# One kernel of graph layers: the projection matrices get a load semaphore of their own, and orders, banks and rows are new

## What is computed

```
x = layernorm(x + L0(x))   # q,k,v = x @ w.T + b; 4 heads; softmax(mask(q k / sqrt(32))) v; @ wo.T + bo
x = layernorm(x + L1(x))   # h = x W; softmax over leaky_relu(s_i + d_j), masked; times h
x = layernorm(x + L2(x))   # the same with 8 heads and a log prior; @ W_out.T
x = layernorm(x + L3(x))   # relu(x w + b); attention of width 256 without mask, elu; relu(x w + b);
                           # attention of width 128 with mask, elu, sums
```

## Time and profile before

| what | value |
|---|---|
| median of 3 runs | 1070.28 us (1068.1, 1070.28, 1076.06) |
| the profiled execution, its own time | 1069.56 us |
| its span, first to last instruction | 1067.7 us |
| TensorE busy | 999.2 us (94%) |
| VectorE busy | 910.9 us (85%) |
| ScalarE busy | 763.6 us (72%) |
| GpSimd busy | 403.2 us (38%) |
| mean granted clock of TensorE | 0.991 |

### The profile page before, as it was taken

The page is one execution under the profiler, slowest core; times in us unless marked ns, Lnnn a source line. Parts: engine busy times, 40 slices in busy tenths (PEclk is TensorE's granted clock), DMA queues, the critical chain, the costliest instruction groups (busy, mean ns, idle before and its releaser), DMA issues. The chain is left out here.

```text
span 1067.7 us, 25731 instructions
## 1 busy us (share of the span) xinstructions
PE 999.2 (94%) x8649; PEld 731.7 (69%) x8649; DVE 910.9 (85%) x2499; ACT 763.6 (72%) x2022; POOL 403.2 (38%) x660
## 2 busy tenths in 40 slices
PE   7999999999999999999999999999999999998995
PEld 4776666775667677676868677776867576856774
DVE  3988998889899798998899999788889996899654
ACT  4789875785888687788877789797866836544653
POOL 1013333250444562434736371653535272320111
PEclk9999999999999999999999999999999999999998
DMA  4001111021212120312203130310202120320000
GB/s 128 2 22 43 60 64 60 21 91 45 68 44 70 52 87 27 102 42 75 73 27 93 41 113 11 92 41 32 82 26 87 32 82 1 101 70 22 11 10 21
DMA packets 41530, 57.89 MB, mean 54 GB/s; under 512 B 12728, under 2 KB 15288, under 8 KB 41400
## 3 DMA queue, kind: packets, MB, share of 16 engines
q1 hardware_dynamic: 40536, 55.98, 17.2%
q10 hardware_dynamic: 864, 0.26, 0.1%
HBM read 51.12 MB, written 5.11 MB: 53 GB/s over the span
## 5 line engine op out<-in xcount | busy, mean ns | idle before, releaser
L1329 DVE SCALAR_TENSOR_TENSOR P<-row,t2e,mask_t 128x512 f32<-128x512 f32 x512 | 367.4, 776 | 13.3 <-PE bank L689 10.9
L856 ACT ACTIVATE probs<-probs,low 128x512 f32<-128x512 f32 x256 | 185.6, 727 | 46.4 <-DVE low L1128 45.5
L1128 DVE CUSTOM_DVE_ANT_0 probs<-bank,mask_add 128x512 f32<-128x512 f32 x256 | 170.1, 675 | 10.2 <-PE bank L582 10.1
L867 ACT ACTIVATE probs_t<-bank 128x512 f32<-128x512 f32 x232 | 136.3, 606 | 19.8 <-PE bank L590 19.4
L590 PE MATMUL bank<-ident,probs 128*128 128x128 f32 x1024 | 139.6, 277 | 7.0 <-ACT probs L856 5.5
L590 PEld LDWEIGHTS bank<-ident,probs 128*128 128x128 f32 x1024 | 112.8, 141 | 44.4 <-ACT probs L856 25.1
L902 ACT ACTIVATE x<-x,shift_l,rstd_l 128x128 f32<-128x128 f32 x256 | 105.3, 487 | 47.9 <-POOL shift_l L1486 47.5
L1471 POOL TENSOR_TENSOR rstd_l<-mv_l,ln_eps 128x4 f32<-128x4 f32 x64 | 19.8, 309 | 303.8 <-DVE mv_l L1197 303.8
L734 PE MATMUL bank<-t,l_P 128*128 128x258 f32 x512 | 119.3, 387 | 4.9 <-DVE low L1128 2.1
L689 PE MATMUL bank<-P,GH 128*32 128x512 f32 x1024 | 118.2, 602 | 4.5 <-issue 2.3
L734 PEld LDWEIGHTS bank<-t,l_P 128*128 128x128 f32 x512 | 95.9, 192 | 20.9 <-DVE low L1128 2.3
(11 more groups left out here) (179 smaller groups left out, 1958.3 us busy)
## 6 DMA issues: line engine op xcount, KB each, us to landing
row<-l_line SPq DMA_DIRECT2D x158, 256.0 KB, 3.8
x_in<-in_x SPq DMA_DIRECT2D x16, 256.0 KB, 2.6
out<-x SPq DMA_DIRECT2D x15, 256.0 KB, 2.0
row<-l3b_line SPq DMA_DIRECT2D x10, 256.0 KB, 3.0
l_P<-in_adj SPq DMA_DIRECT2D x4, 256.0 KB, 4.5
l_line<-turned SPq DMA_DIRECT2D x26, 16.0 KB
l_line<-l_turned SPq DMA_DIRECT2D x20, 16.0 KB
w_fc<-in_L_gnn_W_fc SPq DMA_DIRECT2D x1, 256.0 KB, 3.8
```

Source lines behind the costliest of these rows:

```text
L856: act.activation(e, e, ACT.Exp, bias=low0[:, m:m + 1], scale=-1.0, accum_out=g.of(den0)[:, m:m + 1])\
L867: act.activation(probs_t[c % 2][:, h, :, :].rearrange("p j n -> p (j n)"), ps("l0_t", g, m)[:, :], ACT.Copy)\
L1128: dve.tensor_tensor_reduce(probs[c % 2][:, h, :], ps("l0_s", g, m)[:, :], mask_add[:, c, :], 1.0, LOWEST, ALU.add, ALU.min, low0[:, m:m + ...
L1329: last = dve.scalar_tensor_tensor(P2[:, h % GROUP2, j, :], row("l2_spread", g, h)[:, :], g.of(t2e)[:, j, h:h + 1], mask_t[:, j, :], ALU.ma ...
```

## The change

The three matrices are loaded first, then the bias of q, the bias of k, and the bias of v. `proj_in` now counts only the three matrices, and TensorE's `proj_T` waits for those three. The biases of q and k count on a new semaphore, which ScalarE waits for ahead of scaling the bias of q; the bias of v counts on another, which VectorE waits for in `l0_v` of graph 0.

The tables `ORDER`, `BANK_OF_USE` and `ROW_OF_USE` are replaced. Each string has the same turns as before, except that TensorE has 63 warm-up turns where it had 65. A warm-up turn now stands on both sides of `proj_T`. The first 12 turns of ScalarE, 6 of VectorE, 18 of GpSimd and 15 of SyncE are unchanged, and so are the last 163 of TensorE (41 of them warm-up turns), 122 of ScalarE, 151 of VectorE, 33 of GpSimd and 21 of SyncE. The kernel has no table of durations, so only the orders show that part of the change. The diff, with some lines of two of the strings and without the rest of the tables:

```diff
--- before.py
+++ after.py
     "pe":
-        "Z0Z0a010Z0b0c0d0e0e0f0f0f0a1f020b1c1f0e0g0f0f0d1Z0Z0Z0Z0Z0Z0Z0Z0Z0000000f000Z0e0f0f0g0f0f0e1f0g0f0f0"
...
-        "b4c4g3t0f3f3u0f3f3d4o1j2p1p1k2e4g3q1k2f4e4f4Z0r1t0f4f4e4u0f4l2f4f4i3v0f4e4w0g4f4f4f4f4g4a5g4f4b5c5d5"
-        "f4x0Z0Z0j3y0y0k3k3f4t1l3z0z0z0z0n2f4A0u1e5g4n2f5B0i4f5f5t1Z0u1C0o2f5C0C0p2p2C0j4e5q2k4k4v1g5r2w1D0n3"
...
-        "ybrdFaFaffzbzbzbzbefffffffAbfftcGagfgfucffffffvcffwcnegfhfneifZ0Z0tdCbxcCbCbCbjfJakfkfudJaoetdDbpepe"
-        "DblfIaudEbycycmfFbFbzczczcqezcreGbvdAcwdnfBcnfZ0Z0CcxdCcCcCcZ0Z0Z0Z0ofJbpfpfJbDcDcqfZ0terfIbEcydydue"
...
+        "Z0Z0a0Z010Z0b0c0d0e0e0f0f0f0a1f020b1f0c1e0f0g0f0d1Z0Z0Z0Z0Z0Z0Z0Z0Z0000000f000g0e0f0f0f0f0e1f0g0f0f0"
...
+        "f3d4f3t0g3f3f3u0f3j2o1e4p1p1f3k2k2f4g3q1e4f4f4f4t0r1e4u0i3f4l2f4f4v0f4g4w0e4f4f4f4f4j3g4k3k3f4x0a5g4"
+        "f4y0y0l3f4f4z0z0z0g4b5z0t1A0n2c5u1n2i4e5B0d5f5f5Z0Z0Z0C0C0C0o2C0p2p2e5f5f5q2t1r2e5j4f5u1f5f5k4k4f5v1"
...
+        "ffffzbzbzbzbefgfAbfffffffftcgfgfucffffffffGaZ0gfhfvcZ0wcneneiftdCbxcCbCbCbjfJakfkfudJatdDboeDblfudpe"
+        "peIaEbycycmfFbFbzczczcqezcreGbvdAcwdnfBcnfZ0Z0CcxdCcCcCcZ0Z0Z0Z0ofJbpfpfJbDcDcqfZ0terfIbEcydydueFcFc"
...
     "dve":
-        "00a0b0b0b0b0c00020b0c0b030b04010b050c0a10060b0c0b000b0b0c0b0b0b0c0b0b1b1b1c0d0c0e0b1b1b1b1f0b1c1c1g0"
...
+        "00a0b0b0b0b000c0b020c0b030b04010b0c050a100c0b060b000b0b0b0c0b0b0c0b0b1b1b1c0d0c0e0b1b1b1b1f0c1b1c1g0"
...
@@ -328,7 +328,7 @@
         row_filled = [sem(f"row_filled{r}") for r in range(ROWS)]
         x_loaded = [sem(f"x_loaded{q}") for q in range(2)]
         stored = [sem(f"stored{q}") for q in range(2)]
-        for name, n in [("proj_in", 6 * 16), ("out_in", 3 * 16), ("l1_in", 2 * 16), ("l2_in", 4 * 16), ("l3_in", 9 * 16), ("add_mask", C), ("one_mask", 1),
+        for name, n in [("proj_in", 3 * 16), ("bias_qk_in", 2 * 16), ("bias_v_in", 16), ("out_in", 3 * 16), ("l1_in", 2 * 16), ("l2_in", 4 * 16), ("l3_in", 9 * 16), ("add_mask", C), ("one_mask", 1),
                         ("fold1", 1), ("fold2", 1), ("fold3", 1), ("prior_in", 1), ("prior_exp", 1), ("prior_ln", 1),
                         ("prior_out", 1), ("x_biased", 1), ("bias_q_made", 1), ("exp0", 16), ("den0_safe", 1), ("rden0_made", 1),
                         ("l2_c4", 1), ("dmax8_diag", 1), ("small2_made", 2), ("exp2", 3), ("gh2", 1), ("rden2_made", 2), ("p2_made", HEADS2),
@@ -762,7 +762,7 @@
                 last.then_inc(filled("l3_r", g), 1)
 
             stages = {
-                "mask_T": mask_T, "proj_T": turn_raw("proj_T", ("wq", "wk", "wv"), "proj_in", 6 * 16),
+                "mask_T": mask_T, "proj_T": turn_raw("proj_T", ("wq", "wk", "wv"), "proj_in", 3 * 16),
                 "out_T": turn_raw("out_T", ("wo", "w_out"), "out_in", 3 * 16), "l0_xT": to_T("l0_xT", lambda g: g.of(x_in), lambda g: pe.wait_ge(g.of(x_loaded), 16 * (g.i // 2) + 16)),
                 "l0_q": l0_qk("q"), "l0_k": l0_qk("k"), "l0_v": l0_v, "l0_s": l0_s, "l0_t": l0_t, "l0_pv": l0_pv,
                 "l0_rd": l0_rd, "l0_y": l0_y,
@@ -795,13 +795,11 @@
         @block.scalar
         def _(act):
             def proj_load(g, k):
-                loaded = signal["proj_in"]
-                for n, key in (("wq", "L0_gnn_wq"), ("wk", "L0_gnn_wk")):
-                    act.dma_start(rawf[:, RAW[n] * D:(RAW[n] + 1) * D], w[key]).then_inc(loaded, 16)
-                act.dma_start(bias_q[:, 0:1], w["L0_gnn_bq"].rearrange("(p o) -> p o", o=1)).then_inc(loaded, 16)
-                act.dma_start(bias_k[:, :], w["L0_gnn_bk"].rearrange("(p o) -> p o", o=1)).then_inc(loaded, 16)
-                act.dma_start(rawf[:, RAW["wv"] * D:(RAW["wv"] + 1) * D], w["L0_gnn_wv"]).then_inc(loaded, 16)
-                act.dma_start(bias_v[:, :], everywhere(w["L0_gnn_bv"], D)).then_inc(loaded, 16)
+                for n, key in (("wq", "L0_gnn_wq"), ("wk", "L0_gnn_wk"), ("wv", "L0_gnn_wv")):
+                    act.dma_start(rawf[:, RAW[n] * D:(RAW[n] + 1) * D], w[key]).then_inc(signal["proj_in"], 16)
+                act.dma_start(bias_q[:, 0:1], w["L0_gnn_bq"].rearrange("(p o) -> p o", o=1)).then_inc(signal["bias_qk_in"], 16)
+                act.dma_start(bias_k[:, :], w["L0_gnn_bk"].rearrange("(p o) -> p o", o=1)).then_inc(signal["bias_qk_in"], 16)
+                act.dma_start(bias_v[:, :], everywhere(w["L0_gnn_bv"], D)).then_inc(signal["bias_v_in"], 16)
                 act.preload_act_table_set("natural_log_exp_and_others")
 
             def raw_out(stage, names):
@@ -814,7 +812,7 @@
 
             def proj_t(g, k):
                 raw_out("proj_T", ("wq", "wk", "wv"))(g, k)
-                act.wait_ge(*sig("proj_in", g, 6 * 16))
+                act.wait_ge(*sig("bias_qk_in", g, 2 * 16))
                 act.activation(bias_q[:, 1:2], bias_q[:, 0:1], ACT.Copy, scale=-SCALE0).then_inc(signal["bias_q_made"], 1)
 
             def mask_t_out(g, j):
@@ -1110,6 +1108,8 @@
 
             def l0_v(g, k):
                 dve.wait_ge(*wrote("l0_v", g))
+                if g.i == 0:
+                    dve.wait_ge(*sig("bias_v_in", g, 16))
                 if g.has(2):
                     dve.wait_ge(*wrote("l0_pv", g, C - 1, back=2))
                 dve.tensor_tensor(g.of(v0)[:, :, :], ps("l0_v", g)[:, :].rearrange("p (c n) -> p c n", c=C),
```

More of the change, by code:

```diff
@@ L65 @@
[L65 to L74, removed]
@@ new lines @@
+        "peIaEbycycmfFbFbzczczcqezcreGbvdAcwdnfBcnfZ0Z0CcxdCcCcCcZ0Z0Z0Z0ofJbpfpfJbDcDcqfZ0terfIbEcydydueFcFc"
+        "zdzdzdzdZ0AdGcZ0Z0Z0BdZ0Z0teCdCdCdCdueHcZ0Z0Z0Z0vewetfDdDdufJcJcxeIcZ0EdyeyeFdFdzezezezetfAeGdufBeHd"
+        "vfwfZ0Z0Z0Z0CeCeCeCexfJdJdIdDeDeZ0EeyfyfFeFezfzfzfzfGeZ0AfHeBfZ0Z0Z0Z0Z0Z0JeCfCfCfCfJeIeZ0DfDfZ0Z0Ef"
+        "FfFfGfZ0Z0HfZ0Z0Z0Z0Z0Z0JfJfIf",
+    "act":
+        "90a020b0c0d0d0e0d0d0e0a1d030b1e0d0c1d0f0e0d00010000000d0f0d0d0e0d0e0d0d0d0e0d0f0d1e0d1d1e1d1f0d1d1e1"
+        "d1d1e1d1e1d1f1e1g0d1a2f1d1e1h0d1b2d1i0d1i0e1d1c2f1e1j0d2f1d2d2d2e2e2d2d2l0d2d2l0e2d2e2d2g1d2e2h1f2e2"
+        "d2m0i1f2i1d2n0d2e2o0f2o0a3d2d2b3j1c3e2p0d3d3f2e3d3e3d3e3d3e3d3d3e3e3f3e3d3e3d3l1f3d3e3a4e3d3l1b4d3e3"
+        "c4e3d3g2d3d3r0m1e3f3e3h2n1e3d3o1d4o1i2e3i2e4f3d4d4d4e4e4e4d4d4d4d4r0p1d4d4e4e4t0e4d4e4j2f4d4g3e4d4h3"
+        "e4u0i3e4i3e4d4e4v0f4d4e4w0f4d4w0e4a5e4x0x0j3x0f4b5x0r1c5l2y0l2d5d5e5e5d5m2A0d5A0n2A0o2o2A0e5d5e5d5g4"
+        "d5r1d5p2h4d5e5d5i4e5i4e5t1e5d5j4B0f5C0d5d5d5d5d5e5e5e5e5u1D0l3f5l3v1e5E0e5E0f5w1w1e5e5a6x1x1x1f5m3b6"
+        "x1r2n3c6o3o3y1d6d6e6e6a7b7d6p3d6g5F0A1A1A1h5A1c7B1C1r2i5H0t2H0d6I0i5e6J0e6d6d6d6e6u2l4D1l4d6v2d6d6d6"
+        "r3w2K0w2E1e6E1e6x2m4x2e6x2j5n4x2d6f6o4o4e6e6d6e6d6e6y2e6f6e6d6p4e6f6e6d7d7d7d7r3F1f6d7e7d7e7d7e7e7e7"
+        "d7e7e7d7d7e7A2d7d7A2H1g6A2H1t3h6A2e7I1d7J1d7i6d7f7d7u3r4l5B2C2l5i6e7v3e7e7f7e7e7f7e7e7a8f7b8c8m5n5d8"
+        "D2d8w3d8w3o5g7o5x3j6K1x3h7x3d8x3d8i7E2e8E2e8i7p5d8y3d8d8r4e8e8j7F2e8d8e8d8e8d8e8f8d8t4e8e8d8e8e8f8f8"
+        "e8u4A3d8v4l6H2l6A3e8d8d8A3A3H2B3m6C3I2n6e8r5o6e8o6J2a9f8b9c9D3w4w4E3E3x4g8x4d9x4d9x4e9d9h8F3d9K2i8p6"
+        "r5y4i8d9e9d9e9d9e9d9e9e9d9e9d9e9t5e9d9e9f9d9aae9j8H3d9H3d9I3bae9J3d9u5A4l7v5l7A4d9A4A4B4C4r6m7caK3e9"
+        "f9e9n7f9e9e9o7o7f9D4w5w5E4E4x5x5x5g9x5F4dadadadar6h9y5p7i9dai9daeadaeadaeat6eaabj9eaeaeaeaH4daH4I4bb"
+        "J4dadacbdau6dal8A5l8A5dav6daA5daA5faB5eaC5eaeaeam8dbK4dbn8dbfar7eafaeao8dbo8D5w6w6E5E5eax6x6x6x6eadb"
+        "fadbebdbeby6ebF5ebdbebdbebdbebp8ebgar7dbdbhadbaciaiadbbcdbccdbH5fbebjaA6H5I5J5A6A6A6ebB6ebC6ebt7dcdc"
+        "r8K5D6dcfbu7ebl9E6l9E6ebv7ebfbebdcw7ecw7ecfbececx7x7x7x7m9n9y7dcdcgbo9dco9r8hbdcF6dcibdcibecdcp9t8jb"
+        "ecfcecdcecadbddcH6dcH6u8A7I6A7lav8laA7J6A7ecB7ecC7ecfcecdcecdcecmar9cdfcnaecoaoaD7w8w8E7E7ecx8x8x8fc"
+        "x8K6ddy8ddF7ddr9ddddedddedddt9paedddedddgcddedededddedhcfdddH7ddu9H7lbI7lbA8ddA8v9J7ddA8icA8edB8mbC8"
+        "edicedfdedddK7raedfdednbededobobaefdjcbeD8w9w9E8E8x9x9x9cex9gddey9dedepbradeF8deeedeeedeeetaeehddeee"
+        "eeeeeeiddefededededeA9deualcA9lcH8vadeA9deA9B9eeC9eeH8eemceeI8rbfeJ8feeeeenceeeeococfeD9wawaE9E9xaxa"
+        "xaxaidF9geK8hepcrbieyaiejdafbftbcfjedfH9dfH9I9J9efefubldldvbAaAadfAamdAaefndBadfCadfrcodK9odefdfdfef"
+        "dfefdfDadfwbdfwbEapdEaefdfxbefxbxbxbffdfefdfybefdfefdfefrcffffefefefefFafftcucrdlegfAblevcAbAbhfAbif"
+        "HaifBbmeCbHaIaJardneoeoejfDbwcwcEbKaxcEbxcxcxctdFbpeycudlflfvdAcAcBcCcAcmfAcBcnfCcofofHbHbIbJbreDcwd"
@@ L153 @@
+        "g5b8c8g5aaj3l2k3f6h4g6i4g6g6g6d8e8g6g6g6b9c9g6l3abj4k4h5f7i5g7g7d9e9g7g7g7g7g7g7bacal4h6acj5i6k5f8g8"
+        "g8g8g8bbdacbeag8g8g8g8l5adh7i7j6k6f9dbg9ebg9g9g9g9g9g9g9ael6h8j7i8k7fagagagagagagagal7gaafh9fbi9j8gb"
+        "k8gbgbgbgbgbgbgbj9k9l8fchagciagcgcgcgcgcgcgcl9fdgdhbgdibgdgdjagdkagdgdgdlajbfekbgegegegegegegegeffgf"
         "gflbgfgfgfgfgfgflcldlelf",
```

143 lines of the change are left out of this document (62 added, 81 removed).

## The result

| kernel | median, us | lowest to highest | own time of the profiled execution | its span | clock |
|---|---|---|---|---|---|
| before | 1070.32 | 1068.1 to 1076.06 | 1069.56 | 1067.7 | 0.991 |
| changed | 1078.92 | 1076.39 to 1082.79 | 1076.39 | 1074.6 | 0.991 |

The ratio is 1.0075, with a 95% interval of 1.0047 to 1.0102: some 8 us slower, where 7 us faster was forecast. Both the sign and the range (to 1072) were wrong. The median of before is over four runs here, one more than in the table of the time before.

The account below looks back on a forecast made before the run. The prediction took TensorE, with small stalls, to bound the kernel. It summed 1069.56 - 2.35 (head) - 1.75 (clock) - 2.5 (orders) = 1062.96, with half of 0.72 1063.3, and said 1063.5 us; range for 8 in 10, 1055.5 to 1072.

Parts of the forecast that it names:

- The head: Start of the kernel: L531 no longer waits for bias_v and starts at 7.5 instead of 9.85, 2.35 us won.
- The clock: q and k of graph 0 run at full clock: 1.75 us won, bounds 0 and some 0.5 more.
- Rival 1: The clock stays down over q and k in the head: 1065.2 us, chance 0.15.
- That the head's gain arrives: After the head, VectorE's nearly unbroken list moves up with graph 0's scores, so 4.1 us are won.
- Rival 3: The head's gain is eaten or the separate semaphore does nothing for the end: 1066 to 1070 us, chance 0.17.
- Orders, banks and rows: Some 800 us of the body are reordered and the drain kept: -2.5 us, bounds -11 to +10.
- I take -2.5, with -11 to +10 as the bounds: Reordered body: -2.5 us; -11 is all three stalls and their dips gone, +10 four stretches like 100 to 150 more.
- a scatter around nothing: Body's idle drawn anew in 16 stretches, spread estimated at 1.4 us each, so their sum scatters by 5.6 us.
- The list of large stalls: Three stalls named as the body's largest: 1.45 us at 164.22, 2.08 at 399.36 and 2.05 at 890.08.
- the visible gains: Body: 1.9 us behind the first large stall and 2.05 us at the third, 3.95 us won, more if dips go.
- Rival 4: VectorE becomes the bound where layer 1 of graph 8 is moved: slower, 1075.7 us with four such stretches, chance 0.12.

Follow-up runs that it names:

- e1_loads: The kernel before with only the change's loads and semaphores, all orders, banks and rows kept: 1063.37 us, ratio 0.9966 to the kernel before.
- e10_bba: The kernel before with the new loads, its old orders to 721 us and the new orders after: 1062.62 us, ratio 0.9952 to the kernel before.
- e2_old_loads: The kernel before with the new order, bank and row tables, its loads and semaphores kept: 1078.21 us, ratio 1.0110 to the kernel before.
- the four later swaps: Further edits of GpSimd's order in the changed kernel: ratio to the kernel before 1.0051 with one swap, 1.0061 with three, 1.0071 with five.

## Why the prediction was wrong, point by point

*The head: right.* L531 at 7.49 (forecast 7.5), no wait for bias_v; q at 8.86 (9.2); v's sum at 11.74 (12), second mask step at 15.24 (15.6). The scores of graph 0 start 4.4 us sooner (4.1). e1_loads has the gain alone at the end of the kernel: 3.7 us. The bias of v landed at 8.84, not at 9.79.

*The clock: right.* q and k took 1.10 and 1.02 us, so it had risen by q. Part of the turning of the matrices was at the higher level already (0.58 us for what took 0.90), 0.3 of the 0.5 more that the bounds held. TensorE's work from 2.2 to 8.5 was unbroken, and two of its pieces are transposes (5.78 to 6.63, and 7.49 to 7.90). Rival 1 falls. The Trainium skill ("TensorE: Matmul & The Clock Gate", section "Part 4: PE-mode transpose") has it that TensorE's transpose mode doesn't count as busy in the same way. I drew from it that these transposes would break the run and that q would take 2.04; the trace disagrees with that. Its rows don't tell whether they ran in the mode that is meant there.

The other runs bear the result out, but not my reason for it. In all 15 profiles with the new loads q took 1.10 to 1.16 us, and in both with the old loads, which make TensorE wait ahead of L531, 2.04 and 1.72. But I had argued from the trace of before, where the work from 2.2 to 6.8 hadn't raised the clock. In e1_loads the same matmuls and transposes had raised it by 6.2 us: the last two transposes of x came 0.11 us apart, as did those of L531, where the first two came 0.21 apart. In e10_bba matmuls still came 0.21 apart at 7.7. So the moment differs between executions, and the one trace of before couldn't tell it.

*That the head's gain arrives: right*, by e1_loads and by e2_old_loads against the changed kernel. Rival 3 falls.

*Orders, banks and rows: wrong.* The step that failed is "I take -2.5, with -11 to +10 as the bounds". The orders cost +11.7 us (1.0075 against 0.9966). Two things were wrong in it. I priced the stalls that the trace of before shows, and took what 900 moved turns bring as a scatter around nothing. It was a bias: beside the 15 us that the middle loses stand 12 us more of waits at two hand-overs of GpSimd, a term that the sum didn't have, and with these products halved the orders draw level to about 4 us. And the scatter came from a spread that I had assumed. The list of large stalls had a gap as well: between 50 and 850 the second largest was 1.51 us at 716.57, ahead of the 1.45 at 164.22. Even the visible gains came in only in part: the stall of 164 us and its dip are gone, but a wait for x of 2.00 us still stands at 932.42, where 2.05 stood at 890.08, and the granted clock drops for 3.4 us four times instead of three. One of these is shown in a window behind the stall at 465.01:

```profile
465.00:468.00 3.00, 2.99 (x7) 2.43 (x8) 1.19 (x4) 1.59 (x6) 1.96 (x4) 0.51 0.60 205
```

*Rival 4* had the sign, 0.12 of chance and 1075.7 us, but the wrong engine and place: I gave it to VectorE at layer 1 of graph 8. VectorE's busy time in 50 to 850 is less than before (708.44 against 716.78). I had read GpSimd's 38% in the earlier trace rows as an engine without a say. What stood in the trace of before and would have warned: between the end of a graph's last `l3_p` and the start of its `l3_o` there were 0.05 to 0.5 us for five of the graphs 2 to 11 (after: 0.05 to 0.5 for seven). For three of the five (graphs 7 to 9, at 0.05) TensorE was waiting already, by 0.87, 0.44 and 0.20 us. At such a hand-over a move of TensorE's `l3_o` forward, or of GpSimd's turns back, goes straight into a stall.

*What stays open.* That the new orders wait at GpSimd's hand-overs, and that they draw level to about 4 us once its products are halved, is shown. Which moved turns make the hand-overs late isn't: the four later swaps on GpSimd gave nothing, no run changed what brings the rows late, and GpSimd's old string was not tried with the other engines' new ones. Of the remaining 3 us of the middle's 15 some may be the clock: between 91 and 721 us it fell three times (at 103, 465 and 622) where it had fallen twice, and the prediction read 1.7 us from one such fall. The rest I can't put down to one wait.

## What to carry to other kernels

An engine's share of busy time says nothing of its slack: at 38%, most of a loss of 12 us hung on GpSimd, as its few long products end just before TensorE reads them. Look one step behind a wait, too: three of the stalls named after GpSimd were rows that it waited for itself. Before a written-out order is changed, list for each hand-over the time from the producer's end to the consumer's start, for the idle engines too, and count the ones near nothing as places where a new order can only lose. And a change of two parts is best timed as two kernels: the loads were worth 3.7 us, and the tables hid it.
